# One graph-attention layer on one core: selection by copies under marks, bases in PSUM, and a new order of VectorE's pass

## The chip, the cores and the metric

The kernel runs on one core of a Trainium2 chip. The time is the device time of one execution in microseconds (us); the median of several runs is compared. Engines: PE is TensorE, DVE is VectorE, ACT is ScalarE, POOL is GpSimd, SP is SyncE. L1068 is line 1068 of the kernel before.

## The reference, cut to what matters

There are 6250 nodes of 96 values (four heads of 24) and 106250 edges. Every node is the source of at least one edge (its loop); the edges come sorted by `dst`, not by `src`, and sums are taken by `src`.

```python
q = (embeds[rows] @ qW).reshape(e, HEADS, dh)      # rows = src
k = (embeds[cols] @ kW).reshape(e, HEADS, dh)      # cols = dst
v = (embeds[cols] @ vW).reshape(e, HEADS, dh)
scores = jnp.clip(jnp.einsum('ehd,ehd->eh', q, k), -10.0, 10.0)
exp_s = jnp.exp(scores)
norms = jax.ops.segment_sum(exp_s, rows, num_segments=nvar)[rows]
w = exp_s / (norms + 1e-08)
res = jax.ops.segment_sum(w[:, :, None] * v, rows, num_segments=nvar).reshape(nvar, d)
# the layer gives embeds + res; the output is layernorm(x + layer(x))
```

## The kernel before

**Tiles.** The nodes form 49 bins of 128. The edges are sorted by bin of `src` on the chip, so that a tile of 128 edges touches one bin. Five tiles (U = 5) make a pass. There are 176 passes' worth of work (NBT); I call the five tiles of one pass "tile n" below, n from 0 to 175. For tile n POOL gathers the k and v rows of its edges from HBM, five indirect DMAs (L510), into one of eight buffers. TensorE turns one-hot matrices (L678) and multiplies them with the q table (L652); VectorE multiplies q by k (L1210), reduces per head (L1230), clips (L1238); ScalarE takes the exponential (L768); VectorE weighs v (L1220); TensorE sums the edges into their nodes with the one-hot (the residual product, L666); VectorE adds the five results to `acc` at the bin's row (`add_up`, L1191). The row comes from five block numbers, which VectorE loads into registers from SBUF (`blocks_of`, L425).

**Groups.** The edges come in six groups (140, 110, 130, 150, 160, 160 columns of 125 edges). While the tiles of one group are worked on, the next group is ranked and sorted, in pieces that the same engines take in between. Group 0 goes first and alone. Ranking a group with C columns has K = C / 10 columns per strip and these pieces on VectorE: `mark0` to `mark3` (49 compares that mark the edges of each bin, `steps_m`, L871), `pair0` to `pair2` (rank within the edge's strip), `count`, `base0` and `base1` (scans that give each bin's first position, `kb_m`, L1045), `bounds`, `sel0` to `sel6`, `table`, `tree`, `own` and `choose`. The selection (`select`, from L1054) finds for each edge the base of its bin: the marks of seven bins at a time are multiplied by their bases (L1068) and the seven products are summed (L1065), so seven products and six sums of 7 C elements; `tree` sums the seven rows that are left. `own_position` (L1085) makes from it the position in the tile (`held[:, 2]`), the step position (`pos_h` in fp16, `pos_t` in fp32, L1098 to L1100), and for groups 1 to 5 copies three payload rows to the PSUM bank `ps_b` (L1097). Sorting then takes units of ten columns (`unit`, L1103): a ramp compare (L1121), a one-hot of the place (L1125), and two products with the payload (L1129, L1132), which TensorE sums.

**Order.** The planner (`plan`, L107) writes the order out for every engine. For groups 1 to 5 the passes m = -2 to 120 are shared out: the passes that rank carry ranking pieces after the tile work, the passes that sort carry one unit, at times two, and two passes at each group's end carry neither. Group 1 has 6 passes that rank (m = -2 to 3) and 8 that sort, group 2 has 8 and 11, group 3 has 10 and 13, group 4 has 11 and 16, group 5 has 12 and 18. The selection of group 4, for instance, lies in the passes 66 to 69, two blocks in each and the last alone. From m = 121 on the passes have tile work only; the tiles 125 to 134 come in pairs that share one gather.

**A pass on VectorE** (`tiles`, L1180) at number m loads the block numbers of tile m-2, multiplies tile m (waits for the gather and for q), weighs tile m-1 (waits for the exponential), waits for the residual product of tile m-2, and then adds tile m-2, with the reduction, the one-hot of tile m+2 (L1199) and the clip between the additions. Each addition waits for the one before it, since both may have the same row. In a pass that ranks, the additions are taken by `add_one`, one behind each step of a piece that asks for it (`link` issues an instruction, takes one addition along and waits for the instruction's end); what is left is added at the end of the pass.

**POOL** issues the gathers of tile n when buffer n is free (tile n-8 has been weighed, L505) and the residual product of tile n-6 is done (L507; not for the tiles 125 to 134), and a group's first when the group has been sorted (L501). 

Of the kernel before, what the change touches and what calls it, by code (L numbers as in the profile page):

```python
# [6 lines left out]
def gnn(nc, x, src, dst, qW, kW, vW, out):  # L7
# [6 lines left out]
    P = 128  # L14
# [135 lines left out]
    with ExitStack() as ctx:  # L150
# [13 lines left out]
        pos_h = sb("pos_h", [EP, CMAX], f16)  # L164
# [26 lines left out]
        held = sb("held", [EP, 3, CMAX], f16)  # L191
# [5 lines left out]
        place_m = sb("place_m", [EP, max(28 * CMAX, 6 * P * SU)], u16)  # L197
        kst_m = sb("kst_m", [EP, NB * (KMAX + 2)], f16)
        kb_m = sb("kb_m", [EP, NB * (KMAX + 2)], u16)
# [34 lines left out]
        held_b = ps_b_m[0:EP, :].bitcast(f16)[:, 0:3 * CMAX].rearrange("p (i c) -> p i c", i=3)  # L234

        def payload(g):

            return [(held_b if g else held)[:, i, 0:GC[g]] for i in range(3)]
# [62 lines left out]
        ps_p = ps_r + ps_t  # L301
        ps_last = [ps_r[(NBT - 1) % R % 2]] + ps_q + ps_t
# [176 lines left out]
        def _(pool):  # L479
# [7 lines left out]
            last.then_inc(s_times, 1)  # L487
            nc.gpsimd.memset(dif[:, :, :], 0.0).then_inc(s_zero, 1)
# [325 lines left out]
        def _(dve):  # L814
# [36 lines left out]
            def group_views(g):  # L851
                C, K = GC[g], GK[g]
                return (C, steps_m[0:EP, 0:NB * C].rearrange("p (b c) -> p b c", b=NB),
                        place_m[:, 0:28 * C].rearrange("p (b c) -> p b c", c=C),
                        kst_m[:, 0:NB * (K + 2)].rearrange("p (b k) -> p b k", b=NB),
                        kb_m[:, 0:NB * (K + 2)].rearrange("p (b k) -> p b k", b=NB))

            def mark(g, i):
# [11 lines left out]
                for b in range(NB * i // 4, NB * (i + 1) // 4):  # L870
                    last = nc.vector.tensor_scalar(steps[:, b, :], bin_u[:, 0:C], float(b), None, ALU.is_equal)  # L871
                if i == 3:
                    last.then_inc(s_mark, 1)
# [164 lines left out]
            def base(g, i):  # L1038

                K = GK[g]  # L1040
                n = 4 if K > 20 else 2
# [5 lines left out]
                if i:  # L1047
                    link(last)
                else:
                    add_one()  # L1050

            chosen = {}

            def select(g, i):  # L1054
# [4 lines left out]

                def rows(k):  # L1060
                    return pl[:, 0:n, :] if k == 0 else pl[:, n * (1 + k % 3):n * (2 + k % 3), :]

                def add(k):
                    dve.wait_ge(s_own, max(chosen[0], chosen[k]))
                    chosen[0] = step(nc.vector.tensor_tensor(rows(0), rows(0), rows(k), ALU.add))  # L1065
                    add_one()

                chosen[i] = step(nc.vector.tensor_tensor(rows(i).rearrange("p b (j k) -> p b j k", k=K),  # L1068
                                                         steps[:, bs, :].rearrange("p b (j k) -> p b j k", k=K),
# [312 lines left out]
```

## Time and profile before

| what | us |
|---|---|
| median of three runs (lowest, highest) | 1250.57 (1249.82, 1255.41) |
| the profiled execution: its own time | 1251.4 |
| the profiled execution: its span | 1249.6 |
| first gather begins | 88.93 |
| VectorE busy | 1028.5 |
| POOL busy | 883.9 |
| TensorE busy | 968.9 |

The profile is of one execution; the span runs from its first to its last instruction, and times in the rows count from its start. Busy time is that of an engine's instructions alone; register loads and waits don't count. "issue" is time in which an engine waited for nothing that the profile shows. PEclk is the TensorE clock that was granted, in parts of full speed.

### The profile page before, as it was taken

What the parts mean: (1) busy time and instruction counts of PE and PEld (TensorE: products, weight loads), DVE (VectorE), ACT (ScalarE), POOL (GpSimd) and SP (SyncE); (2) the same over time, 40 slices, a digit from 0 to 9 for tenths busy, and PEclk for the clock granted to TensorE, in tenths of its full rate; (3) what the DMA queues carried; (4) which work ended last, traced back from release to release, by engine and by line L of the source; (5) the groups of instructions that cost most, each with busy time, mean ns of one, the idle gap of its engine ahead of it and who ended that gap; (6) DMA issues with size and microseconds to landing.
All of it is one profiled execution on the core that took longest, in us unless ns stands there. A gap on an engine that the chain in (4) does not pass through costs nothing.

```text
span 1249.6 us, 22903 instructions
## 1 busy us (share of the span) xinstructions
PE 968.9 (78%) x6512; PEld 880.5 (70%) x6513; DVE 1028.5 (82%) x3139; ACT 615.4 (49%) x1328; POOL 883.9 (71%) x887
## 2 busy tenths in 40 slices
PE   8876787688886888768988867889777787888870
PEld 6765676578775887657888756788667677777760
DVE  7999898899989999888999887999766765555557
ACT  7852584248732598222887322788433332222225
POOL 1317777777777777777777777777777777777752
PEclk9996699659975699775899665899867866555555
DMA  6202222222222222222222222222522222222222
GB/s 174 89 9 71 77 80 74 66 74 80 78 77 70 77 78 77 73 77 70 77 78 79 71 76 73 78 77 80 152 76 80 77 76 78 77 79 76 79 61 77
DMA packets 67240, 98.33 MB, mean 79 GB/s; under 512 B 33127, under 2 KB 53204, under 8 KB 67134
## 3 DMA queue, kind: packets, MB, share of 16 engines
q0 software_dynamic: 41040, 84.10, 24.6%
q1 hardware_dynamic: 26094, 12.94, 3.7%
q8 instruction: 51, 0.84, 0.3%
q14 instruction: 55, 0.45, 0.1%
HBM read 89.77 MB, written 7.22 MB: 78 GB/s over the span
## 4 chain that ended last, share of the span: by engine, by line
DVE 43%; issue 18%; POOL 16%; PE 13%; DVEq 7%; ACT 2%; DMA 1%; SPq 0%; POOLq 0%; ACTq 0%
POOL kv L510 16%; DVE acc L1191 10%; DVEq L425 6%; DVE prod L1210 5%; DVE place_m L1125 4%; PE ps_r L666 4%; DVE wv L1220 4%; DVE score L1230 2%; PE ps_q L652 2%; DVE steps_m L871 2%; DVE place_m L1132 2%; PE ps_a L635 2%; DVE place_m L1129 1%; DVE ohb L1199 1%; DVE clipped L1238 1%
## 5 line engine op out<-in xcount | busy, mean ns | idle before, releaser
L510 POOL DMA_INDIRECT kv<-kv_table,dst_s x855 | 858.5, 1004 | 303.6 <-issue 299.1
L666 PE MATMUL ps_r<-wv,oneh 128*128 128x100 f32 x1752 | 328.3, 354 | 104.1 <-DVE wv L1220 103.1
L652 PE MATMUL ps_q<-qt,onehT 128*128 x1760 | 316.9, 344 | 100.5 <-ACT onehT L775 93.9
L666 PEld LDWEIGHTS ps_r<-wv,oneh 128*128 128x128 f32 x1752 | 298.0, 260 | 127.9 <-DVE wv L1220 125.7
L652 PEld LDWEIGHTS ps_q<-qt,onehT 128*128 128x128 f32 x1760 | 289.1, 252 | 124.1 <-issue 124.0
L727 ACT ACTIVATE steps_m<-iota_f,pos_t 125x254 f16<-125x254 f32 (+4 forms) x652 | 255.9, 482 | 12.1 <-PE ps_b L635 8.6
L1191 DVE TENSOR_TENSOR acc<-acc,ps_r 128x100 f32 x876 | 220.1, 251 | 29.4 <-PE ps_r L666 3.6
L1210 DVE TENSOR_TENSOR prod<-ps_q,kv 128x480 f32<-128x480 f32 x176 | 115.0, 653 | 153.8 <-DMA kv<-kv_table,dst_s 91.2
L775 ACT ACTIVATE onehT<-ps_t 128x640 f32<-128x640 bf16 x176 | 124.0, 705 | 217.9 <-PE ps_t L678 211.4
L768 ACT ACTIVATE wv<-clipped 128x20 f32<-128x20 f32 x176 | 38.5, 219 | 351.1 <-DVE clipped L1238 350.7
L781 ACT ACTIVATE oneh<-ohb 128x640 f32<-128x640 bf16 x176 | 164.5, 935 | 0.9 <-PE ps_r L666 0.9
L635 PE MATMUL ps_a<-steps_m,place_m 125*128 125x254 f16 (+4 forms) x1220 | 151.3, 266 | 0.0
L635 PEld LDWEIGHTS ps_a<-steps_m,place_m 125*128 125x128 f16 x1220 | 133.3, 138 | 1.4
L1220 DVE TENSOR_TENSOR wv<-kv,wv 128x480 f32<-128x480 f32 x176 | 114.0, 648 | 2.5 <-issue 2.2
L1230 DVE TENSOR_REDUCE score<-prod 128x20 f32<-128x480 f32 x176 | 113.3, 644 | 0.5 <-PE ps_r L666 0.4
L678 PE MATMUL ps_t<-ident_bf,ohb 128*128 128x128 bf16 x880 | 103.6, 264 | 5.6 <-DVE ohb L1199 5.1
L678 PEld LDWEIGHTS ps_t<-ident_bf,ohb 128*128 128x128 bf16 x880 | 87.2, 139 | 16.5 <-DVE ohb L1199 14.7
L1199 DVE TENSOR_TENSOR ohb<-iota_t,loc_s 128x640 bf16<-128x640 bf16 x176 | 96.6, 549 | 0.0
L635 PE MATMUL ps_a<-theta_g,place_m 125*128 125x254 f16 (+3 forms) x284 | 56.1, 279 | 17.5 <-ACT steps_m L727 17.5
L1129 DVE TENSOR_TENSOR place_m<-place_m,ps_b 125x1280 f16<-125x1280 f16 x71 | 57.7, 813 | 0.2
L1125 DVE TENSOR_TENSOR place_m<-iota_s,ps_b 125x1280 f16<-125x1280 f16 x71 | 57.7, 812 | 0.0
L1132 DVE TENSOR_TENSOR place_m<-place_m,ps_b 125x1280 f16<-125x1280 f16 x71 | 57.6, 811 | 0.0
(212 smaller groups left out, 692.9 us busy)
## 6 DMA issues: line engine op xcount, KB each, us to landing
kv<-kv_table,dst_s POOLq DMA_INDIRECT x855
kv_table<-kv SPq DMA_DIRECT2D x7, 672.0 KB, 3.4
acc<-in_x_dram SPq DMA_DIRECT2D x6, 336.0 KB, 8.4
steps_m<-in_x_dram SPq DMA_DIRECT2D x6, 336.0 KB, 5.2
out_dram<-kv SPq DMA_DIRECT2D x6, 336.0 KB
dst_i<-in_dst_dram SPq DMA_DIRECT2D x1, 415.0 KB
src_i<-in_src_dram SPq DMA_DIRECT2D x1, 346.7 KB
acc<-in_x_dram SPq DMA_DIRECT2D x1, 288.0 KB, 4.4
```

The source lines that it names most:

```text
L510: nc.gpsimd.indirect_dma_start(kv[:, nm, u, :], None, kv_dram, bass.IndirectOffsetOnAxis(ap=dst_s[:, n * U + u:n * U + u + 1], axis=0)).th ...
L635: mm = nc.tensor.matmul(to[:, 0:w], lhs[:, vm, :, j], steps, start=first and j == 0 and (g == 0 or lhs is lhs_a), stop=last and j == SU - ...
L652: last = nc.tensor.matmul(ps_q[nm % 2][:, u * D:(u + 1) * D], onehT[:, nm % 2, u * P:(u + 1) * P], qt[:, bass.ds(blks[u], 1), :].rearrange ...
L666: last = nc.tensor.matmul(to, oneh[:, nm % 2, u, :], wv[:, nm % 2, u, :], start=True, stop=True)
L678: last = nc.tensor.transpose(ps_t[nm % 2][:, u * P // 2:(u + 1) * P // 2].bitcast(bf16), ohb[:, nm % 4, :, u], ident_bf[:, :])
L727: last = nc.scalar.activation(theta[:, vm, j, 0:w], iota_f[0:EP, 0:w], ACT.Sign, scale=-1.0, bias=pos_t[:, bass.ds(v * SU + j, 1)])
L775: nc.scalar.activation(onehT[:, nm % 2, :], ps_t[nm % 2][:, 0:U * P // 2].bitcast(bf16), ACT.Copy).then_inc(s_oneT, 1)
L781: nc.scalar.activation(oneh[:, nm % 2, :, :], ohb[:, nm % 4, :, :].rearrange("p n u -> p u n"), ACT.Copy).then_inc(s_onf, 1)
L1191: nc.vector.tensor_tensor(at, at, from_ps, ALU.add).then_inc(s_acc, 1)
L1210: nc.vector.tensor_tensor(prod[:, nm % 2, :].rearrange("p (u d) -> p u d", u=U), ps_q[nm % 2][:, 0:U * D].rearrange("p (u d) -> p u d", u= ...
L1220: nc.vector.tensor_tensor(wv[:, nm % 2, :, 0:D].rearrange("p u (h d) -> p u h d", h=HEADS), kv[:, km, :, D:2 * D].rearrange("p u (h d) -> ...
L1230: nc.vector.tensor_reduce(score[:, nm % 2, :], prod[:, nm % 2, :].rearrange("p (h d) -> p h d", d=DH), axis=AX.X, op=ALU.add).then_inc(s_s ...
```

## The change

- The selection no longer multiplies seven times and adds six times. The first seven bins' marks are multiplied by their bases as before; for the other six blocks the bases are copied into the same seven rows where a mark is set (`copy_predicated`). Each is followed by `link`, so it takes one addition along. `place_m` becomes smaller.
- After the scans, `base1` copies the bases (whole 4-byte words) from `kb_m` to the PSUM bank `ps_b`; the selection reads them there. `kb_m` is set to 0 on POOL once, near the start, and VectorE's wait for it moves from `differ` to `base0` of group 0.
- The step positions (`pos_h`) become a fourth payload row, which for groups 1 to 5 is read from `ps_b`. The copy of the payload comes after it has been made.
- In `mark` every fifth compare takes one addition along, not in the last.
- The pass: the load of the block numbers and the wait for the residual product come after multiply, weigh and reduce (in a pass that ranks, after the one-hot and the clip as well). In a pass that sorts, the additions stand after the load, one each after it, the one-hot, the clip, the place compare and the first place product.

```diff
--- before.py
+++ after.py
@@ -161,7 +161,6 @@
         iota_i = sb("iota_i", [P, IW], i32)
         iota_f = sb("iota_f", [P, IW], f32)
         iota_s = sb("iota_s", [P, P, SU], f16)
-        pos_h = sb("pos_h", [EP, CMAX], f16)
         iota_g = sb("iota_g", [P, TMAX + 1, KG], f16)
         theta_g = sb("theta_g", [EP, 2, TMAX + 1, KG], f16)
         iota_u = sb("iota_u", [P, NB], u16)
@@ -188,15 +187,15 @@
         dst_i = sb("dst_i", [EP, EC], i32)
         tmp_i = sb("tmp_i", [EP, CMAX], i32)
         bin_u = sb("bin_u", [EP, CMAX], u16)
-        held = sb("held", [EP, 3, CMAX], f16)
+        held = sb("held", [EP, 4, CMAX], f16)
         pos_t = sb("pos_t", [EP, EC], f32)
 
         rank_u = sb("rank_u", [EP, CMAX], u16)
         same_u = sb("same_u", [EP, 3, CMAX], u16)
         steps_m = sb("steps_m", [P, max(NB * CMAX, 2 * NPC * PC * D)], f16)
-        place_m = sb("place_m", [EP, max(28 * CMAX, 6 * P * SU)], u16)
+        place_m = sb("place_m", [EP, max(7 * CMAX, 6 * P * SU)], u16)
         kst_m = sb("kst_m", [EP, NB * (KMAX + 2)], f16)
-        kb_m = sb("kb_m", [EP, NB * (KMAX + 2)], u16)
+        kb_m = sb("kb_m", [EP, (NB * (KMAX + 2) + 1) // 2 * 2], u16)
         cnt_f = sb("cnt_f", [EP, NB], f32)
         cnt = sb("cnt", [EP, NB], f16)
         step_i = sb("step_i", [EP, NB], i32)
@@ -231,11 +230,11 @@
 
         ps_b_m = pb("ps_b", [P, 512], f32)
         LW = P * SU
-        held_b = ps_b_m[0:EP, :].bitcast(f16)[:, 0:3 * CMAX].rearrange("p (i c) -> p i c", i=3)
+        held_b = ps_b_m[0:EP, :].bitcast(f16)[:, 0:4 * CMAX].rearrange("p (i c) -> p i c", i=4)
 
         def payload(g):
 
-            return [(held_b if g else held)[:, i, 0:GC[g]] for i in range(3)]
+            return [(held_b if g else held)[:, i, 0:GC[g]] for i in range(4)]
 
         lhs_m = place_m[:, 0:6 * LW].bitcast(f16)
         lhs_1 = lhs_m[:, 0:2 * LW].rearrange("p (i q c) -> p i q c", i=2, c=SU)
@@ -299,6 +298,7 @@
         ps_q = [pb(f"ps_q{i}", [P, 512], f32) for i in range(2)]
         ps_r = [pb(f"ps_r{i}", [P, 512], f32) for i in range(2)]
         ps_p = ps_r + ps_t
+        assert 2 * CMAX <= 512 and NB * (KMAX + 2) < 1024
         ps_last = [ps_r[(NBT - 1) % R % 2]] + ps_q + ps_t
 
         s_x = [sem(f"s_x{i}") for i in range(4)]
@@ -485,6 +485,7 @@
                 nc.gpsimd.memset(times_f[:, k:k + 1], float(a))
                 last = nc.gpsimd.memset(plus_f[:, k:k + 1], float(b))
             last.then_inc(s_times, 1)
+            nc.gpsimd.memset(kb_m[:, :], 0)
             nc.gpsimd.memset(dif[:, :, :], 0.0).then_inc(s_zero, 1)
             def copy_q(i):
                 pool.wait_ge(s_prjc, PC * (i + 1))
@@ -851,9 +852,9 @@
             def group_views(g):
                 C, K = GC[g], GK[g]
                 return (C, steps_m[0:EP, 0:NB * C].rearrange("p (b c) -> p b c", b=NB),
-                        place_m[:, 0:28 * C].rearrange("p (b c) -> p b c", c=C),
+                        place_m[:, 0:7 * C].rearrange("p (b c) -> p b c", c=C),
                         kst_m[:, 0:NB * (K + 2)].rearrange("p (b k) -> p b k", b=NB),
-                        kb_m[:, 0:NB * (K + 2)].rearrange("p (b k) -> p b k", b=NB))
+                        ps_b_m[0:EP, :].bitcast(u16)[:, 0:NB * (K + 2)].rearrange("p (b k) -> p b k", b=NB))
 
             def mark(g, i):
 
@@ -869,6 +870,8 @@
                     link(nc.vector.tensor_scalar(flip[:, 0:C], flip[:, 0:C], float(P - 1), None, ALU.mult))
                 for b in range(NB * i // 4, NB * (i + 1) // 4):
                     last = nc.vector.tensor_scalar(steps[:, b, :], bin_u[:, 0:C], float(b), None, ALU.is_equal)
+                    if b % 5 == 4 and b < NB - 1:
+                        add_one()
                 if i == 3:
                     last.then_inc(s_mark, 1)
 
@@ -1038,6 +1041,8 @@
             def base(g, i):
 
                 K = GK[g]
+                if g == 0 and i == 0:
+                    dve.wait_ge(s_zero, 1)
                 n = 4 if K > 20 else 2
                 for q in range(n * i // 2, n * (i + 1) // 2):
                     b0, b1 = NB * q // n, NB * (q + 1) // n
@@ -1046,35 +1051,24 @@
                                                         0.0 if b0 == 0 else endp[0:EP, b0 - 1:b0], ALU.add, ALU.max)
                 if i:
                     link(last)
+                    words = (NB * (K + 2) + 1) // 2
+                    link(nc.vector.tensor_scalar(ps_b_m[0:EP, 0:words].bitcast(i32), kb_m[:, 0:2 * words].bitcast(i32), 0,
+                                                 None, ALU.bitwise_or))
                 else:
                     add_one()
-
-            chosen = {}
 
             def select(g, i):
 
                 C, steps, pl, _, kb = group_views(g)
                 K, n = GK[g], NB // 7
                 bs = slice(n * i, n * (i + 1))
-
-                def rows(k):
-                    return pl[:, 0:n, :] if k == 0 else pl[:, n * (1 + k % 3):n * (2 + k % 3), :]
-
-                def add(k):
-                    dve.wait_ge(s_own, max(chosen[0], chosen[k]))
-                    chosen[0] = step(nc.vector.tensor_tensor(rows(0), rows(0), rows(k), ALU.add))
-                    add_one()
-
-                chosen[i] = step(nc.vector.tensor_tensor(rows(i).rearrange("p b (j k) -> p b j k", k=K),
-                                                         steps[:, bs, :].rearrange("p b (j k) -> p b j k", k=K),
-                                                         kb[:, bs, 1:K + 1].unsqueeze(2).to_broadcast([EP, n, H, K]),
-                                                         ALU.mult))
-                add_one()
-                if i > 1:
-                    add(i - 1)
-                if i == 6:
-                    add(i)
-                    dve.wait_ge(s_own, chosen[0])
+                to = pl[:, 0:n, :].rearrange("p b (j k) -> p b j k", k=K)
+                marks = steps[:, bs, :].rearrange("p b (j k) -> p b j k", k=K)
+                bases = kb[:, bs, 1:K + 1].unsqueeze(2).to_broadcast([EP, n, H, K])
+                if i == 0:
+                    link(nc.vector.tensor_tensor(to, marks, bases, ALU.mult))
+                else:
+                    link(nc.vector.copy_predicated(to, marks.bitcast(u16), bases))
 
             def tree(g):
 
@@ -1090,13 +1084,13 @@
                 link(nc.vector.tensor_tensor(t, pl[:, 0, :], rank_u[:, 0:C], ALU.add))
                 link(nc.vector.scalar_tensor_tensor(s, t, P - 1, flip[:, 0:C], ALU.bitwise_and, ALU.bitwise_xor))
                 link(nc.vector.tensor_copy(held[:, 2, 0:C], s))
+                link(nc.vector.tensor_scalar(t, t, 7, None, ALU.logical_shift_right))
+                link(nc.vector.tensor_scalar(held[:, 3, 0:C], t, 0.5, None, ALU.add))
                 if g:
-                    words = [a.rearrange("p (i c) -> p i c", i=3)[:, :, 0:C // 2]
-                             for a in (ps_b_m[0:EP, 0:3 * CMAX // 2].bitcast(i32),
+                    words = [a.rearrange("p (i c) -> p i c", i=4)[:, :, 0:C // 2]
+                             for a in (ps_b_m[0:EP, 0:4 * CMAX // 2].bitcast(i32),
                                        held[:, :, :].rearrange("p i c -> p (i c)").bitcast(i32))]
                     nc.vector.tensor_scalar(words[0], words[1], 0, None, ALU.bitwise_or)
-                link(nc.vector.tensor_scalar(t, t, 7, None, ALU.logical_shift_right))
-                link(nc.vector.tensor_scalar(pos_h[:, 0:C], t, 0.5, None, ALU.add))
                 nc.vector.tensor_scalar(pos_t[:, c0:c1], t, 0.5, None, ALU.add).then_inc(s_pos, 1)
                 dve.wait_ge(s_pos, g + 1)
 
@@ -1107,7 +1101,7 @@
                 cols = bass.ds(v * SU, SU)
 
                 here = cols if g == 0 else slice(v * SU - C0[g], v * SU - C0[g] + SU)
-                upper, lower, place = payload(g)
+                upper, lower, place, pos_h = payload(g)
 
                 def spread(a):
                     return a[:, here].unsqueeze(1).to_broadcast([EP, P, SU])
@@ -1135,8 +1129,6 @@
             def differ(g):
 
                 T = TS[g]
-                if g == 0:
-                    dve.wait_ge(s_zero, 1)
                 for i, cum in enumerate((cum_a, cum_b)):
                     dve.wait_ge(s_cum, 2 * g + i + 1)
                     nc.vector.tensor_tensor(dif[:, i, 0:T], cum[:, 0:T], cum[:, 1:T + 1],
@@ -1255,16 +1247,16 @@
                     return
                 if isinstance(m, int) and m == NBT - 2:
                     coming[m - 1] = blocks_of(mybir.EngineType.DVE, m - 1)
+                multiply()
+                weigh()
+                reduce()
+                if mid:
+                    build()
+                    clip()
                 if there(m - 2):
                     blks = blocks_of(mybir.EngineType.DVE, m - 2)
-                multiply()
-                weigh()
-                if there(m - 2):
                     dve.wait_ge(s_res, m - 2 + 1)
                 if mid:
-                    reduce()
-                    build()
-                    clip()
                     behind[0] = iter([(add_up, u) for u in range(U)])
                     for piece, g in mid:
                         piece(g)
@@ -1272,17 +1264,16 @@
                         add_up(u)
                     return
                 add_up(0)
-                reduce()
+                build()
                 add_up(1)
-                build()
+                clip()
                 add_up(2)
-                clip()
-                add_up(3)
                 if sorts:
-                    unit(*sorts[0], between=lambda i: None if i else add_up(4))
+                    unit(*sorts[0], between=lambda i: add_up(3 + i))
                     for sort in sorts[1:]:
                         unit(*sort)
                 else:
+                    add_up(3)
                     add_up(4)
 
             follow(dve, tiles, unit, {"count": count, "table": table, "own": own_position,
```

## Rows read from the trace of the kernel before

**Rows 1.** the page, part 1: busy time of each engine

```profile
PE 968.9 (78%) x6512; PEld 880.5 (70%) x6513; DVE 1028.5 (82%) x3139; ACT 615.4 (49%) x1328; POOL 883.9 (71%) x887
```

**Rows 2.** the answer on line L510, POOL: durations, and what POOL waited for

```profile
L510 POOL DMA_INDIRECT kv<-kv_table,dst_s x855: 942/947/4894, 88.9 to 1209.0; - x171
...
  PE ps_r L666: 1.2, 4
```

**Rows 3.** busy time by stretch; engines (instructions), TensorE clock, DMA share, GB/s

```profile
600.00:650.00 50.00, 45.79 (x402) 43.24 (x401) 49.50 (x123) 43.72 (x98) 38.04 (x40) 0.99 0.29 78
...
1100.00:1150.00 50.00, 42.47 (x198) 38.47 (x197) 26.00 (x77) 13.82 (x24) 38.12 (x40) 0.50 0.28 78
```

**Rows 4.** timeline of POOL: start, us, line, what [idle before <-releaser]

```profile
88.93 1.23 POOL L510 DMA_INDIRECT kv<-kv_table,dst_s  x1 [41.19 <-issue]
...
114.69 3.00 POOL L510 DMA_INDIRECT kv<-kv_table,dst_s  x1 [0.31 <-issue]
...
388.49 1.07 POOL L510 DMA_INDIRECT kv<-kv_table,dst_s  x1 [1.08 <-issue]
...
596.64 0.95 POOL L510 DMA_INDIRECT kv<-kv_table,dst_s  x1 [0.30 <-issue]
```

**Rows 5.** timeline of TensorE before 596 us

```profile
592.95 2.45 PE L666 MATMUL ps_r<-wv,oneh 128*128 128x100 f32 x10 [0.72 <-DVE wv L1220]
```

**Rows 6.** timeline of VectorE in group 1's selection

```profile
114.81 1.59 DVE L1068 TENSOR_TENSOR place_m<-steps_m,kb_m 125x770 uint16<-125x770 f16 x3
116.33 0.54 DVE L1065 TENSOR_TENSOR place_m<-place_m 125x770 uint16<-125x770 uint16 x1
116.91 0.66 DVE L1210 TENSOR_TENSOR prod<-ps_q,kv 128x480 f32<-128x480 f32 x1
```

**Rows 7.** line L510 by stretch, the five selections of groups 1 to 5

```profile
747.70:767.10 19.40, 15.31 (x14) 0.50 0.26 70
sum 80.40, POOL 64.83; mean POOL 12.97
```

**Rows 8.** VectorE by line and shape: xcount | busy us, mean ns | idle

```profile
L1068 DVE TENSOR_TENSOR place_m<-steps_m,kb_m 125x1120 uint16<-125x1120 f16 x14 | 11.3, 805 | 0.0
L1065 DVE TENSOR_TENSOR place_m<-place_m 125x1120 uint16<-125x1120 uint16 x12 | 8.8, 731 | 0.0
...
L1068 DVE TENSOR_TENSOR place_m<-steps_m,kb_m 125x980 uint16<-125x980 f16 x7 | 4.9, 728 | 0.0
...
L1045 DVE TENSOR_TENSOR_SCAN kb_m<-kst_m,endp 125x450 uint16<-125x450 f16 x2 | 2.3, 1146 | 0.0
...
L928 DVE TENSOR_REDUCE cnt_f<-kst_m 125x49 f32<-125x784 f16 x2 | 1.9, 963 | 0.0
...
L1097 DVE TENSOR_SCALAR ps_b<-held 125x240 int32<-125x240 int32 x2 | 0.8, 406 | 0.0
```

**Rows 9.** the answer on line L425, VectorE: ns min/median/max

```profile
L425 DVEq TENSOR_LOAD <-blk_s x176: 585/1182/1199, 115.9 to 1209.7; - x176
```

**Rows 10.** waits of VectorE from 109 to 591 us: us in total, times, longest

```profile
DVE prod L1210 <- issue: 22.1, 23, 1.4
```

**Rows 11.** timeline of VectorE in a pass that sorts

```profile
621.05 0.65 DVE L1220 TENSOR_TENSOR wv<-kv,wv 128x480 f32<-128x480 f32 x1
621.61 0.25 DVE L1191 TENSOR_TENSOR acc<-acc,ps_r 128x100 f32 x1
621.78 0.64 DVE L1230 TENSOR_REDUCE score<-prod 128x20 f32<-128x480 f32 x1
```

**Rows 12.** timeline of VectorE in a pass that marks

```profile
521.24 2.87 DVE L871 TENSOR_SCALAR steps_m<-bin_u 125x160 f16<-125x160 uint16 x25
524.03 1.85 DVE L1191 TENSOR_TENSOR acc<-acc,ps_r 128x100 f32 x5
```

**Rows 13.** timeline of VectorE, a pass with two selection blocks and the next

```profile
563.40 0.66 DVE L1210 TENSOR_TENSOR prod<-ps_q,kv 128x480 f32<-128x480 f32 x1 [1.07 <-issue]
...
570.62 0.66 DVE L1210 TENSOR_TENSOR prod<-ps_q,kv 128x480 f32<-128x480 f32 x1 [1.06 <-issue]
```

## Prediction

> **What bounds the kernel now.** I read the page's busy shares first, then the gathers' line, then stretches of 50 us, and last single instructions. No engine is busy all the time, VectorE 82%, POOL 71% [rows 1]. But POOL's 855 gathers stand behind one another from 88.9 to 1209.9 us, 947 ns each by the median, with 0.30 us of issue between them; they waited for TensorE 1.2 us in all [rows 2]. 855 x 1.25 is 1069 of those 1121 us. So POOL is full, though its share doesn't say so. In front of it lie 88.9 us (group 0 is ranked and sorted), behind it 39.7 us (last tiles, layer norm).
>
> From 600 to 650 us VectorE is busy 49.5 us of 50 as well; from 1100 to 1150 only 26 [rows 3]. Two full engines side by side are possible because POOL may run at most six tiles ahead of the residual product: L507 waits for it. At 388.49 a gather starts 1.08 us late [rows 4]; tile 76's first gather starts at 596.64, and the product that it needs (tile 70's) ended at 595.40 [rows 4, 5]. So up to about 600 us the kernel has **two bounds**, POOL and VectorE's passes, 1.2 us apart. After that POOL alone sets the end. The sum is therefore made at tile 76: what VectorE's passes gain or lose up to there, less 1.2 us if they lose, and then what POOL gains behind it.
>
> **What stops POOL.** A gather that starts while VectorE runs an instruction with both inputs in SBUF ends late: the one at 114.69 took 3.00 us [rows 4], under three products and one sum of the selection, and it ended 0.8 us after the last of these, under a multiplication that reads PSUM [rows 6]. In the five stretches of selection 54 gathers took 64.83 us, 54 x 0.947 is 51.1, so 13.7 us too much, 2.1 of it in the last group [rows 7]; with the 3.00 us one that is 15.8. The change takes these inputs out of SBUF. The Trainium skill (SBUF — State Buffer, "Who interferes with whom") says that a tensor_tensor takes only the read interface and that descriptor generation needs the write one, so that it doesn't stall a DMA. By that rule this part would be worth nothing; the rows disagree, and the trace decides. But I count in full only the 2.1 us behind tile 76, since before it VectorE is the bound as well.
>
> **The parts, on VectorE's path to tile 76** (passes 1 to 71: 33 that sort, 32 that rank, 6 in between).
>
> Register load moved. L425 loads five block numbers, 1182 ns by the median, 585 at least [rows 9]. Before, in a pass that sorts, it stood behind the last two place products (0.81 us each) and cost nothing: no idle time in the pass at 621, and 49.5 of 50 us busy [rows 3, 11]. Now it stands behind the reduction. The reduction can be issued when the multiplication is done, 0.66 us after the pass began, so the load starts at 0.74 and ends at 1.92; the addition behind it, with its own register work (0.14 us idle between two additions in a row, and another wait), can start at 2.14. The engine is through with weighing and reduction at 1.78, as each follows the last after 0.57 [rows 11], and the addition would have started at 1.70. A long load costs 0.44 us, a short one nothing; I take three long in four, 0.33 x 33 = **+10.9 us**. Bounds: 0 (all covered) and 0.9 (the load starts only with the reduction).
> In a pass that ranks it was open already: up to 591 us VectorE was idle 22.1 us in 23 places before the multiplication [rows 10]; in others the additions covered it. Now it stands behind the clip, with only the one-hot and the clip over it, so it is open in every such pass: 0.9 us a long one, 0.3 a short one, less where the first piece waits anyway; 0.65 x 32 + 0.3 x 6 is 22.6. **+0.5 us**.
>
> Additions between the marks. Five in a row took 1.85 us, 0.37 each; between other instructions one costs 0.17 (0.25 less the 0.08 by which neighbours overlap) [rows 11, 12]. 1 us in one pass of each of groups 2 to 4: **-3 us**. One mark in five followed by an addition also opens the block of 25 for POOL.
>
> Selection. Before, with 16 columns: 7 products of 805 ns and 6 sums of 731 [rows 8], with the overlap 7 x 0.72 + 6 x 0.65 = 8.9 us. Now one product and 6 copies. No row shows a predicated copy. The ends are 2 elements a cycle, as the sums have it (0.73 us for 1120), and 2.2 ns an element, as the scan has it (1146 ns for 450), so 2.5 us. I take one element a cycle, as the fp16 reduction has it (963 ns for 784, also no plain tensor_tensor): 1120 / 0.96 + 150 ns = 1.32 us, 1.23 behind a neighbour. The Trainium skill (Vector Engine (DVE) Microarchitecture Reference, 5.1) lists copy, cast, tensor_scalar and tensor_tensor as those with the faster modes and no predicated copy; that agrees. So 0.72 + 6 x 1.23 = 8.1, and moving the bases to PSUM, 441 words, by the row of 240 words in 406 ns, 0.62: 8.7 together, 0.2 less. But each block now takes one addition along, not two, and two more per pass stand in a burst at its end, 0.2 each, in 10 passes: +4. For four groups **+3 us**. A pass of two blocks took 7.22 us with its open load at the end [rows 13]; the same count gives 7.15 after.
> Group 0 has no additions to take along: 7 products of 0.73 less the overlap [rows 8] and 6 sums a tenth shorter are 8.1 us, one product, 6 copies of 1.21 with their waits and the move 8.5: 0, within 0.5. The memset of the bases on POOL, before POOL's first wait for a copy, and VectorE's wait on it: 0. The fourth payload row: 80 words more, 0.08 us a group: 0. Step positions in PSUM: the multiplication with one input there takes 0.66, the one without 0.65 [rows 6, 11]: 0.
> Fewer stops in group 1's selection bring its first tiles' data earlier: **-1 us**.
>
> Sum to tile 76: 10.9 + 0.5 - 3 + 3 - 1 = +10.4; POOL sees +9.2. Behind it: group 5's selection no longer stops POOL, -2.1, nor do its marks, -1.1. Group 5's ranking, where VectorE loses against POOL once more, could stop it again; of such waits there are 1.2 us in all, so nearly none there [rows 2], so 0 to +2, taken as 0. Behind tile 125 POOL sets the pace alone [rows 3]: 0. End: **+6 us** on the profiled execution's 1251.4. That execution lies 0.8 above the median of the runs, 1250.6, so **1256.5** on their scale.
>
> **Rivals.**
> A, the copies run at two elements a cycle. For: 2-byte types throughout, and sums and marks do it. Against: reduction and scan don't. 24 copies on the path are each 0.58 us shorter, -12 with what POOL can follow, and group 0 starts the gathers 3 us earlier: 6 - 12 - 3 = -9, and 1241.5.
> B, the slower side: the load starts when the reduction starts, at 1.14 + 0.05, not when it has been issued. Place: L1259, in each of 33 passes that sort. Price: 0.44 us more for a long one, 0.3 for a short one, 0.4 x 33 = +13: 1269.5. It decides as soon as the pass grows beyond 6.3 us, POOL's own time for a tile. Against it: in the pass at 621 the engine went from one place product to the next without a gap, so it was given work ahead.
> C, the load is covered in the sorting passes after all (it is mostly short, or the additions catch up): -10.6 on VectorE, of which POOL follows some 7: 1249.5.
> D, VectorE is no bound, POOL takes the whole relief, 15.8 and 3 us at the marks: 1232. Against it: the late gathers [rows 4].
> That the copy holds the port like the product did would take back the 2.1 us and little else, so it changes no case.
>
> **Numbers.** This kernel's runs can tell about 0.5% (6 us) from nothing: faster is below 1244.3, slower above 1256.8. Forecast 0.45, own range 1250 to 1262; A 0.22; B 0.12; C 0.13; D 0.03; a copy slower than an element a cycle, or worse, 0.05. Faster: 0.18 of A, D, 0.04 of C and the rest: 0.25. Slower: 0.2 of the forecast's own spread, B, 0.03: 0.35. Same: 0.40. The range 1239 to 1266 leaves out D, half of B and the slow copy.
>
> **What would show it.** In the profile after: predicated copies of about 1.3 us (0.73: A); passes that sort 6.1 us apart instead of 5.76, with 0.4 us idle before the first addition (0.9: B; none: C); no gather above 1.5 us in the stretches of selection; the issue idle before the multiplication gone from the ranking passes and found again behind the clip; POOL waiting for the residual product several us in all before 600 us, and none after 800. If gathers wait nowhere and the end is earlier by 15 us, my two bounds were wrong.

## The result and the profile after

The changed kernel took **1260.26 us** (median of 6 runs, 1258.07 to 1260.71) against 1251.20 for the kernel before on the same chip; the ratio is **1.0065**, 95% interval 1.0047 to 1.0083. So it is slower by 0.65%: inside the range of the forecast (1239 to 1266), 3.8 us above its value, on the side to which it gave 0.35. What the runs below show is that the sum was nearly right because two of its terms were wrong in opposite directions, the pass by about 8 us and the selection by about 10.

The page after, its first lines:

```profile
span 1258.2 us, 22848 instructions
...
PE 960.0 (76%) x6512; PEld 873.6 (69%) x6513; DVE 1049.5 (83%) x3109; ACT 615.2 (49%) x1328; POOL 857.4 (68%) x888
```

The gathers (now L511) and what POOL waited for, in us and times:

```profile
L511 POOL DMA_INDIRECT kv<-kv_table,dst_s x855: 940/946/2366, 90.7 to 1217.4; - x171
...
  DVE dst_s L1159: 6.9, 2
  PE ps_r L667: 4.9, 2
```

POOL's own work shrank by 26.5 us (883.9 to 857.4, [rows 1]) and the longest gather fell from 4.89 us to 2.37 [rows 2], yet the last gather starts 8.4 us later. The relief of POOL was real and did not reach the end. Gathers are 22.2 us shorter in all (by their time above 0.945 us each, 50.6 before and 28.4 now), but POOL's idle time before them grew by 29.2 us, from 303.6 to 332.8: 7.9 of that is put down to the residual product and the sorted block numbers, the larger part, 21.3, to "issue". The late starts, each at the first gather of a tile and most of them 0.5 to 2.5 us, lie before 610 us and at 796.5 and 803.4; behind that there are none. I read it so that VectorE sets POOL's pace up to 610 us; for the 21.3 us the profile names no one.

The costs of the parts, by line (xcount | busy us, mean ns | idle before):

```profile
L1183 DVE TENSOR_TENSOR acc<-acc,ps_r 128x100 f32 x876 | 222.9, 254 | 71.4 <-issue 35.8 <-DVE acc L1183 3.2 <-PE ps_r L667 1.1
L1202 DVE TENSOR_TENSOR prod<-ps_q,kv 128x480 f32<-128x480 f32 x176 | 114.8, 652 | 76.6 <-DMA kv<-kv_table,dst_s 71.2 <-PE ps_q L653 4.6
...
L1071 DVE COPY_PREDICATED place_m<-steps_m,ps_b 125x1120 uint16<-125x1120 uint16 x12 | 15.8, 1321 | 3.4 <-issue 3.4
...
L1055 DVE TENSOR_SCALAR ps_b<-kb_m 125x441 int32<-125x441 int32 x2 | 1.2, 615 | 0.0
```

The copy takes 1.32 us and the move 0.62, both as forecast. The issue idle is gone from before the multiplication, 46.5 us in the kernel before, and 35.8 of it stand before the additions. A pass that sorts, on VectorE's timeline:

```profile
440.56 0.65 DVE L1202 TENSOR_TENSOR prod<-ps_q,kv 128x480 f32<-128x480 f32 x1
441.13 0.65 DVE L1212 TENSOR_TENSOR wv<-kv,wv 128x480 f32<-128x480 f32 x1
441.69 0.65 DVE L1222 TENSOR_REDUCE score<-prod 128x20 f32<-128x480 f32 x1
442.66 0.26 DVE L1183 TENSOR_TENSOR acc<-acc,ps_r 128x100 f32 x1 [0.32 <-issue]
442.84 0.55 DVE L1191 TENSOR_TENSOR ohb<-iota_t,loc_s 128x640 bf16<-128x640 bf16 x1
...
446.73 0.65 DVE L1202 TENSOR_TENSOR prod<-ps_q,kv 128x480 f32<-128x480 f32 x1
```

6.17 us from multiplication to multiplication, 5.76 in the kernel before (where the load is the short one, mostly in every fourth pass, it is 5.76 still): the load of 1.18 us starts at 441.3, and weighing and reduction cover it only to 442.34. That is the 0.4 us of the forecast, in its place. The stretch of [rows 3] shows the same: VectorE is busy 47.10 us of 50 where it was 49.50.

```profile
600.00:650.00 50.00, 42.83 (x327) 40.00 (x327) 47.10 (x122) 37.52 (x83) 37.45 (x38) 0.83 0.27 74
```

So each single row came out. Whether the sum did for the stated reasons, only undoing its parts can tell.

### The profile page after: what moved, and what is told of

Its sections match the earlier page's. It is cut to its first block, busy times and chain, and to the rows that moved or that the text cites. A ratio compares the mean times of both kernels' runs of the same rounds, so it can differ in the third digit from the quotient of the medians.

```text
span 1258.2 us, 22848 instructions
## 1 busy us (share of the span) xinstructions
PE 960.0 (76%) x6512; PEld 873.6 (69%) x6513; DVE 1049.5 (83%) x3109; ACT 615.2 (49%) x1328; POOL 857.4 (68%) x888
## 4 chain that ended last, share of the span: by engine, by line
DVE 46%; issue 20%; POOL 13%; PE 13%; DVEq 5%; ACT 2%; DMA 1%; SPq 0%; POOLq 0%; ACTq 0%
POOL kv L511 13%; DVE acc L1183 10%; DVE prod L1202 6%; DVE place_m L1119 5%; DVE wv L1212 4%; DVE place_m L1126 4%; PE ps_r L667 3%; DVEq L425 3%; PE ps_q L653 2%; DVE ohb L1191 2%; DVE steps_m L872 2%; DVE score L1222 2%; PE ps_r L548 1%; PE ps_a L636 1%; PE ps_t L548 1%
## 5 line engine op out<-in xcount | busy, mean ns | idle before, releaser
L511 POOL DMA_INDIRECT kv<-kv_table,dst_s x855 | 836.4, 978 | 332.8 <-issue 320.4
L667 PE MATMUL ps_r<-wv,oneh 128*128 128x100 f32 x1752 | 323.2, 350 | 105.3 <-DVE wv L1212 104.9
L653 PE MATMUL ps_q<-qt,onehT 128*128 x1760 | 313.7, 342 | 100.9 <-ACT onehT L776 92.4
L667 PEld LDWEIGHTS ps_r<-wv,oneh 128*128 128x128 f32 x1752 | 293.0, 256 | 127.3 <-DVE wv L1212 123.7
L1183 DVE TENSOR_TENSOR acc<-acc,ps_r 128x100 f32 x876 | 222.9, 254 | 71.4 <-issue 35.8
L679 PE MATMUL ps_t<-ident_bf,ohb 128*128 128x128 bf16 x880 | 102.0, 262 | 17.3 <-DVE ohb L1191 16.9
```

The lines of the kernel that those rows point to most:

```text
L511: nc.gpsimd.indirect_dma_start(kv[:, nm, u, :], None, kv_dram, bass.IndirectOffsetOnAxis(ap=dst_s[:, n * U + u:n * U + u + 1], axis=0)).th ...
L653: last = nc.tensor.matmul(ps_q[nm % 2][:, u * D:(u + 1) * D], onehT[:, nm % 2, u * P:(u + 1) * P], qt[:, bass.ds(blks[u], 1), :].rearrange ...
L667: last = nc.tensor.matmul(to, oneh[:, nm % 2, u, :], wv[:, nm % 2, u, :], start=True, stop=True)
L679: last = nc.tensor.transpose(ps_t[nm % 2][:, u * P // 2:(u + 1) * P // 2].bitcast(bf16), ohb[:, nm % 4, :, u], ident_bf[:, :])
L1183: nc.vector.tensor_tensor(at, at, from_ps, ALU.add).then_inc(s_acc, 1)
```

## The experiments

"Sel" is the selection with bases and step positions in PSUM and the copies, "pass" the new order of VectorE's pass, "marks" the additions between the marks. "Against before" is the ratio less 1, times 1251 us; each set of runs has its own runs of the kernel before beside it (medians 1249.64 to 1251.66), so the ratios are compared, not the times. Idle time of VectorE in a pass is the time from one multiplication's start to the next, less the time in which VectorE is busy, read from the trace.

### One part at a time

**e1_old_pass** (sel and marks):

```diff
-multiply(); weigh(); reduce(); [build(); clip();] load; wait s_res
-add_up(0); build(); add_up(1); clip(); add_up(2); unit(... add_up(3 + i))
+load; multiply(); weigh(); wait s_res
+add_up(0); reduce(); add_up(1); build(); add_up(2); clip(); add_up(3); unit(... add_up(4))
```

> The kernel after, with VectorE's pass put back as before: the register load stands ahead of the multiplication again, the reduction behind the first addition, and only one addition stands inside the sorting unit. Theory 1 (the load's place is what costs): sorting passes fall from 6.17 to 5.76 us, passes without pieces rise from 3.70 or 4.12 to 4.03 or 4.62 us; the sum over the 24 or so long sorting passes is -10 us at VectorE and the time is 8 to 10 us under the kernel after, 1250 to 1252 us, within 0.2% of the kernel before. Theory 2 (the selection with copies and what it does to group 0 costs it): the time stays within 3 us of the kernel after, 1257 to 1261 us.

**e2_new_pass_only**: the same lines the other way round, in the kernel before.

> The kernel before, with only the new order of VectorE's pass. Theory 1: sorting passes at 6.17 us instead of 5.76, time 1259 to 1262 us, since the selection's +3 and the marks' -3 cancel in the kernel after. Theory 2: 1250 to 1253 us.

**e3_selection_only**: e1 with

```diff
-                    if b % 5 == 4 and b < NB - 1:
-                        add_one()
```

> The kernel after with the old pass and without the additions between the marks: bases and step positions in PSUM and the copies under the marks are all that is left of the change. By the prediction's terms: selection +3 on VectorE, earlier data -1, a start that is 1.8 us later (measured in the kernel after), and -2 for gathers that nothing stops: 1251 to 1254 us. Rival (gathers that no longer stop under the products give their whole relief to the end): 1240 to 1245 us, selections of groups 1 to 4 shorter on POOL by 10 us each and kept to the end.

**e4_marks_only**: these two lines in the kernel before.

> The kernel before, with only the additions between the marks. Theory (prediction's term): the wait for ps_r and the idle behind the marks go, -3 on VectorE's path and about -1 on POOL's: 1247 to 1249.5 us. Rival (VectorE's free time stays free, since POOL or the planner's dates hold the pass): 1250.5 to 1252 us.

**e12_no_marks** (sel and pass): the two lines taken from the kernel after.

> The kernel after without the additions between the marks. By the pairs measured so far they are worth 4.1 us on the kernel before and 6.0 us on the changed selection with the old pass. If the parts add up: 1265 to 1267 us. If the new pass already frees residual products in time (its additions come later, so the wait behind the marks is longer instead): 1268 us or more; if they overlap: 1261 to 1263 us.

| | pass | sel | marks | us | ratio (95%) | against before |
|---|---|---|---|---|---|---|
| e4 | | | x | 1246.61 | 0.9961 (0.9947 to 0.9976) | -4.9 |
| e2 | x | | | 1253.31 | 1.0022 (1.0005 to 1.0040) | +2.8 |
| e1 | | x | x | 1255.32 | 1.0032 (1.0020 to 1.0044) | +4.0 |
| after | x | x | x | 1260.26 | 1.0065 (1.0047 to 1.0083) | +8.1 |
| e3 | | x | | 1261.35 | 1.0085 (1.0071 to 1.0098) | +10.6 |
| e12 | x | x | | 1262.56 | 1.0104 (1.0088 to 1.0120) | +13.0 |

The **selection costs +10.6** alone and 13.0 - 2.8 = +10.2 with the new pass. The **pass costs +2.8** alone, 13.0 - 10.6 = +2.4 with the selection, 8.1 - 4.0 = +4.1 with both others. The **marks are worth -4.9**, -6.6 and -4.9. The parts add up: 10.6 + 2.8 - 4.9 = 8.5, measured 8.1. (e12's own expectation for parts that add up, 1265 to 1267, was made in absolute times; the kernel before ran at 1249.64 beside it, and by the ratios 13.0 stands against 10.6 + 2.8 = 13.4.) Of my expectations e1's fell between its two cases (1250 to 1252 and 1257 to 1261), e2's first fell (1259 to 1262) and its second was missed by 0.3 us (1250 to 1253), e3's fell with both of its cases (1254 was the top), and e4 lies 0.4 us below its range. The pass is not the main thing that makes the change slow.

### Why the selection costs ten

VectorE's timeline at the first two blocks of group 2's selection, in the kernel before:

```profile
241.97 1.23 DVE L1068 TENSOR_TENSOR place_m<-steps_m,kb_m 125x910 uint16<-125x910 f16 x2
243.12 0.64 DVE L1210 TENSOR_TENSOR prod<-ps_q,kv 128x480 f32<-128x480 f32 x1
```

and the load beside them:

```profile
L425 DVEq TENSOR_LOAD <-blk_s x1: 1185/1185/1185, 241.4 to 241.4; - x1
```

The same place in e3, with its load:

```profile
244.65 0.64 DVE L1067 TENSOR_TENSOR place_m<-steps_m,ps_b 125x910 uint16<-125x910 f16 x1
245.32 1.11 DVE L1069 COPY_PREDICATED place_m<-steps_m,ps_b 125x910 uint16<-125x910 uint16 x1
247.77 0.66 DVE L1200 TENSOR_TENSOR prod<-ps_q,kv 128x480 f32<-128x480 f32 x1 [1.34 <-issue]
```
```profile
L425 DVEq TENSOR_LOAD <-blk_s x1: 1185/1185/1185, 246.5 to 246.5; - x1
```

In the kernel before a product is issued and nobody waits for it (its sum does, a block later), so the load at 241.4 runs while the products are still queued and costs nothing. In the changed selection each block ends with a wait for its own copy (`link`). The load, next on the sequencer, can start only at 246.5, when the copy is through, and VectorE stands for 1.34 us. Summed over the 15 passes of groups 2 to 5 that hold a block, VectorE's idle time is 12.9 us before and 24.4 in e3, **11.5 us more, and these 15 passes together are 10.9 us longer**; the end was 10.6 later.

**e5_wait_ahead** tests that on e3:

```diff
-                if i == 0:
-                    link(nc.vector.tensor_tensor(...))
-                else:
-                    link(nc.vector.copy_predicated(...))
+                dve.wait_ge(s_own, own[0])
+                ... the same instructions, with step() and add_one()
+                if i == 6:
+                    dve.wait_ge(s_own, own[0])
```

> The old pass and the selection of the change without the additions between the marks (1261.4 us, 10.6 above before), with one thing altered: a copy waits for the copy before it ahead of itself, not behind itself, so that no wait stands behind the last copy of a pass. Theory 3 (formed from the traces): in the kernel before the register load of 1.19 us ran while the last two products of a selection pass were still queued; in the changed selection a wait stands behind the last copy, and the load starts only when the copy is through, 1.5 us of idle VectorE in each of some 8 selection passes. With the wait ahead the load starts with the last copy or addition: idle falls from 1.4 to 1.6 us to under 0.5 us in these passes, 1251 to 1254 us. Rival (copies at one element a cycle, and three small bursts of additions, cost it): 1259 to 1262 us.

Measured 1255.79, ratio 1.0038 (1.0023 to 1.0053): +4.8 against before, 5.8 us less than e3, over half of the +10.6 and not all of it. It lies between the theory's range and the rival's. At the same place:

```profile
243.81 1.10 DVE L1070 COPY_PREDICATED place_m<-steps_m,ps_b 125x910 uint16<-125x910 uint16 x1
245.12 0.66 DVE L1204 TENSOR_TENSOR prod<-ps_q,kv 128x480 f32<-128x480 f32 x1 [0.21 <-issue]
```

The load starts at 243.8, with the copy, and 1.34 us of idle are 0.21. But idle in the 15 passes fell only to 19.8, since most of them end in additions, each of which waits for something, and not in a copy; there the load is nearly as open as in e3 (1.07 us of idle in the next pass, 1.28 in e3). The remaining +4.8 goes with that: these 15 passes are still 6.1 us longer than before. How it divides between the open loads and the copies themselves wasn't tried.

### A load that is covered in every pass

The load wants 1.2 us of work in front of it that was issued without waiting. Weighing, reduction and one-hot are 1.8 us, and the clip, which waits for the reduction, belongs behind it. **e6_load_ahead_of_clip**, on the kernel after:

```diff
 multiply(); weigh(); reduce()
+build()
 load
+clip()
 wait s_res
-[mid: build(); clip() ahead of the load]  add_up(0); build(); add_up(1); clip(); add_up(2)
+add_up(0); add_up(1); add_up(2)
```

> The kernel after with the order multiplication, weighing, reduction, one-hot, load, clip, additions in every pass. Theory 1 (a load is free when over 1.2 us of work is queued ahead of it that waits for nothing late, here weighing, reduction and one-hot, 1.8 us): sorting passes return from 6.17 to 5.76 us, idle in ranking passes falls from 0.9 to under 0.3 us, 1242 to 1248 us. Rival (POOL's chain sets the end by now): 1256 to 1260 us.

**e7_both**: e6 with the wait of e5.

> The same order of the pass, and the copies' wait ahead of them. Theory: the load no longer hangs on the end of a pass, so the place of the wait is worth only its own latency, 0.1 us in each selection pass: 0 to 2 us under the kernel with the load ahead of the clip alone. Rival (the wait at the end of a selection pass costs 1.5 us whatever the order): 8 us or more under it.

e6 took 1239.72 us, ratio 0.9907 (0.9889 to 0.9924), some 20 us under the kernel after and 2 below its range; e7 1236.96, 0.9879 (0.9862 to 0.9897). Idle in the 15 selection passes went from 15.6 us (after) to 9.4 and 8.4, and in the 24 other passes between 12 and 70 that don't sort from 19.1 to 9.8 and 11.2. The rival to e6, that POOL's chain sets the end, fell. In e7 the wait's place is worth about 3 us by the medians (0 to 2 expected), with intervals that overlap. What came out wrong is the sorting pass, 6.07 us and not 5.76, though the load is covered. Its line in e7:

```profile
436.25 0.17 DVE L1234 TENSOR_SCALAR clipped<-score 128x20 f32<-128x20 f32 x1
436.33 1.04 DVE L1187 TENSOR_TENSOR acc<-acc,ps_r 128x100 f32 x3
437.29 0.40 DVE L1119 TENSOR_TENSOR theta_g<-iota_g,ps_b 125x488 f16<-125x488 f16 x1
```

Three additions in a row take 0.96 us to the next instruction, 0.32 each; between other instructions one takes 0.17. **e9_no_bursts**, on e7, for passes without selection or ranking:

```diff
-add_up(0); add_up(1); add_up(2)          (clip ahead)
+add_up(0); clip(); add_up(1)
     unit:  theta ...
+    between(-1)                          (add_up(2))
            lhs_1 ...
```

> The best kernel so far (load behind the one-hot, copies' wait ahead of them, 1237.0 us) had sorting passes at 6.06 us and not at the 5.76 expected: three additions in a row cost 0.22 us more each than additions with other work between them. Here every addition of a sorting pass stands between two other instructions. Theory (VectorE's bursts): sorting passes at 5.76 us and 1231 to 1235 us. Rival (in the sorting stretches VectorE waits for gathers or runs ahead anyway, so nothing of it reaches the end): 1236 to 1238 us.

**1232.16 us**, ratio 0.9858 (0.9841 to 0.9876): 1.4% under the kernel before and the best of all. Sorting passes came to 5.80 us, 5.76 with a short load, in the trace where VectorE doesn't wait for data; from 789 us on they are mostly 6.0 to 6.6, with VectorE waiting for data: before the multiplication it waits 91.0 us in all for gathers (e7 77.4). POOL has become the tighter one there.

### Are the copies worth having?

**e8_bases_in_sbuf** (on the kernel after) and **e10_no_bursts_sbuf** (on e9) read the bases where the scan leaves them:

```diff
-                        ps_b_m[0:EP, :].bitcast(u16)[:, 0:NB * (K + 2)]...
+                        kb_m[:, 0:NB * (K + 2)]...
-                    link(nc.vector.tensor_scalar(ps_b_m[0:EP, 0:words].bitcast(i32), ...))
```

> The kernel after with its selection reading the bases from SBUF, and without the move of the bases to PSUM: product and copies then have marks and bases in SBUF both. Theory (gathers stop under products because both inputs lie in SBUF): the first product alone stops gathers if the copies' mode is what frees them; copies from SBUF stop them too if the place of the inputs decides: then selections of groups 1 to 5 lose some 2 us each on POOL, the move's 0.6 us is saved, and the time is 1259 to 1263 us. If the copies stop no gather wherever the bases lie: 1255 to 1258 us, no gather above 1.2 us under a copy.

> The same, with the bases left in SBUF and no move of them to PSUM. The kernel after became 3.6 us faster by that. Theory (the move and its wait on VectorE's path, 0.9 us in each of five groups, outweigh the gathers that copies from SBUF slow down, 7.6 us in all on POOL): 2 to 4 us under the run with the bases in PSUM. Rival (with VectorE relieved POOL is the tighter one, so the slowed gathers count in full): 0 to 4 us over it.

**e11_products_new_pass**: products and sums of the kernel before, in the pass of e9, with the marks.

> The products and sums of the kernel before, with the additions between the marks and the pass whose load stands behind the one-hot and whose additions stand apart. Theory (the copies cost VectorE more than they give POOL, 4 to 5 us without the exposed loads): 2 to 5 us under the kernel with copies, bases in PSUM and the same pass. Rival (gathers that stop under products cost the end once VectorE is relieved): 3 to 8 us over it.

| | us | ratio (95%) | gathers over 1.5 us | gathers above 0.945 us each, sum |
|---|---|---|---|---|
| before | 1251.20 | 1 | 9 | 50.6 us |
| after | 1260.26 | 1.0065 (1.0047 to 1.0083) | 5 | 28.4 us |
| e8 | 1256.69 | 1.0046 (1.0031 to 1.0061) | 15 | 32.4 us |
| e9 | 1232.16 | 0.9858 (0.9841 to 0.9876) | 5 | 28.3 us |
| e10 | 1238.16 | 0.9908 (0.9893 to 0.9922) | 14 | 34.9 us |
| e11 | 1243.58 | 0.9948 (0.9935 to 0.9961) | 18 | 48.9 us |

The sign turns with the bound. With VectorE as the bound (after, e8) the move to PSUM is a loss of some 2 to 4 us; with VectorE relieved (e9, e10) it gains 6. And the selection with copies, which cost 10.6 us in the old pass (4.8 with the wait ahead of them, as e9 has it), gains **11.4 us** in the pass of e9 over the products of e11. My theories for e10 and e11 fell, and the rivals held in direction and were too small (up to 4 and 8 us). For e8 neither case held whole: the time is that of the copies that stop nothing, and the gathers say otherwise. POOL in e10, and VectorE beside it:

```profile
547.09 0.95 POOL L511 DMA_INDIRECT kv<-kv_table,dst_s  x1 [0.30 <-issue]
548.34 2.03 POOL L511 DMA_INDIRECT kv<-kv_table,dst_s  x1 [0.30 <-issue]
...
554.58 2.04 POOL L511 DMA_INDIRECT kv<-kv_table,dst_s  x1 [0.30 <-issue]
```
```profile
548.24 1.32 DVE L1069 COPY_PREDICATED place_m<-steps_m,kb_m 125x1120 uint16<-125x1120 uint16 x1
```

A gather that starts under a copy with marks and bases in SBUF ends 1.1 us late. The same stretch in e9, six copies from PSUM (1.31 us each) beside it:

```profile
547.09 0.95 POOL L511 DMA_INDIRECT kv<-kv_table,dst_s  x1 [0.30 <-issue]
548.34 0.94 POOL L511 DMA_INDIRECT kv<-kv_table,dst_s  x1 [0.30 <-issue]
...
554.58 0.94 POOL L511 DMA_INDIRECT kv<-kv_table,dst_s  x1 [0.30 <-issue]
```

In e11 POOL is the bound: VectorE waits 116.7 us for gathers before its multiplications, against 91.0 in e9. Counted from its own first gather, and against the kernel before, POOL begins tile 76 10.9 us earlier in e9 and 1.4 later in e11, while VectorE comes to that tile early in both (16.8 and 14.9 us).

Counted over the gathers that overlap a product or a copy of the selection, the late time is 15.8 us before, 0.2 in the kernel after, 8.6 in e8, 0.8 in e9, 14.0 in e10 and 20.1 in e11. The rest of the table's sums, 21 to 35 us, is not the selection's: of the five gathers over 1.5 us in the kernel after, and of the five in e9, two lie under the scans of `base`, two under weighing and reduction, and one under marks.

## Why the forecast's number held and its sum didn't

- **The pass, forecast +10.9 and +0.5, of which POOL was to see 1.2 less; measured +2.8 at the end.** The sorting passes were right: the 37 of them up to tile 75 are 10.7 us longer in e2, and idle in the 56 sorting passes after tile 15 goes from 3.5 to 17.3 us. Two things failed. The first is the +0.5 for the other passes: the 35 passes between 12 and 70 that don't sort became 3.9 us shorter, and their idle went from 34.2 us to 28.4 (from 9.1 to 7.8 in the 11 that hold selection, from 25.1 to 20.6 in the 24 others), so this term is about -4. The multiplication of tile 76 is 6.0 us late, counted from the first gather, and not 11.4. I put one price (0.65) on all 32 passes and set it against the 22.1 us of [rows 10]; by the trace such a pass stood idle for 1.0 us before (34.2 / 35) and 0.8 in e2, and the 22.1 us were only a part of that idle time. Second, what VectorE loses in a sorting stretch is not handed on in full: in e2 the multiplications of tiles 75 and 85 are 5.6 and 9.1 us late, their gathers 4.7 and 4.4 (with the first gather's own 1.4 taken off). There VectorE was faster than POOL, 5.76 us against 6.3, and lost only part of a lead. The step "POOL sees +9.2" fell for this part.
- **The selection, forecast +3, with -1 for earlier data and -2.1 behind tile 76; measured +10.6 alone and +10.2 in the new pass.** The instructions were priced right (1.32, 0.62). The step that failed is the count of what stands between them. In the old pass I had not seen that the two last products of a pass covered the load, 11.5 us of idle. In the new pass idle in the 15 passes is 15.6 us in e12 against 10.8 in e2: I had given +4 to additions in a row, but not seen that each copy now waits for the one before and that the last wait of the pass delays all that is issued behind it. How the rest of the +10.2 divides between that and the additions the runs don't tell.
- **The marks, forecast -3 and -1.1; measured -4.9 alone, -6.6 and -4.9 in company.** Right in size and place: in e4 POOL has gained 2.2 us by tile 75, counted from its first gather, and gains 2.9 more between tiles 90 and 95, where group 5 is marked.
- **Behind tile 76, -3.2.** In the kernel after the gathers went from +11.9 us (tile 76) over +12.6 (tile 90) to +8.7 (tile 105) and ended at +8.4 against before: -3.5 in all, right in size. The waits that I had taken as 0 of "0 to +2" came to 1.5 us, at 796.5 and 803.4.
- **The start.** The first gather is 1.8 us later than before; in the twelve other runs it is 0.2 to 2.1 later, 1.4 in e2, which has neither the memset nor the copies, and 0.2 in e12, which has both. So the term of 0 for group 0 is not shown wrong.
- **The rivals.** A fell with the copies' 1.32 us, B and C with the 0.32 us of idle and the pass of 6.17. D, which I gave 0.03, was wrong for this kernel and half right about the chip: the relief of POOL is worth 11.4 us, but only in e9, once most of VectorE's idle is gone. On the Trainium skill's rule (SBUF — State Buffer, "Who interferes with whom"), by which a tensor_tensor doesn't stall descriptor generation, the runs speak as the rows did, against it: the sum of late time is 48.9 us with products from SBUF (e11) and 28.3 with copies from PSUM (e9), and in the selection alone 20.1 and 0.8.

Against the end the pass was taken some 8 us too dear (+10.2 against +2.8), the selection some 10 too cheap (-0.1 against +10.2 to +10.6) and the marks about right; the sum was +6, measured +8.1 by the ratio. Every row that I had named as proof came out nearly as said; only the runs with single parts showed that the sum was right by chance.

## What to carry to other kernels

A register load that takes 1.2 us on an engine's sequencer is free where work for as long has been issued ahead of it without a wait, and costs its full length behind a wait for one's own last instruction; so when an edit adds a wait at the end of a block, look at what is issued next, and put the wait in front of the instruction that needs it. A relief of the engine that isn't the bound measures as nothing or as a loss: here the selection with copies was worth +10.6 us in the old pass (+4.8 with its waits moved ahead) and -11.4 in the pass of e9, so judge such a part again after the other engine's gaps are closed. Additions that each wait for a semaphore and take their place from a register were cheaper apart (0.17 us) than in a row (0.32); nothing else was tried in a row.

## What the runs showed of the hardware

- A predicated copy of 2-byte elements takes 1321 ns for 1120, 1250 for 1050 and 958 for 770 with the bases in PSUM, and nearly the same with them in SBUF (1324, 1254, 969 in e8): 1.04 ns for each further element.
- It stops gathers by the place of its inputs: with marks and bases in SBUF a gather under it took 2.03 us, with the bases in PSUM 0.94. A single product and sum from SBUF cost less than that (gathers of 1.53 us in the kernel before and in e11); the 4.89 us of [rows 2] came from several, one after another, with additions between them.
- The place of two inputs isn't all of it: the gather of 2.37 us in the kernel after starts at 529.60, and from 529.67 on VectorE runs 13 marks in a row, which read one tensor, in SBUF. What marks and copies have in common wasn't tried.
- Additions in a row leave 0.14 us between one and the next, as [rows 12] had it; what of it is the wait and what the register work for the next address wasn't tried.
